# A four-block kernel on one NeuronCore: unread products on TensorE ahead of two stages, and a small step moved up on VectorE

## What is computed

```python
x = x + attn(moe(x, cond, experts, shared))        # top 2 of 8 experts and a shared one
x = x + ffn_quant(lora(x, cond))                   # quantised gate, up and down projection
x = x + retention(cond_linear(x, cond))
x = x + moe_attention(expert_mlp(x, cond))         # 16 experts by token
```

```python
def _gemma_mlp(x, gate_w, up_w, down_w):
    g = einsum('bsh,hi->bsi', x, gate_w)
    u = einsum('bsh,hi->bsi', x, up_w)
    return einsum('bsi,ih->bsh', gelu(g) * u, down_w)

def act_qdq(x):                                    # 16 bits, one scale for the whole tensor
    scale = maximum(max(abs(x)) / qmax, 1e-12)
    return clip(round(x / scale), -qmax - 1.0, qmax) * scale

x = act_qdq(x)
up = act_qdq(x @ lpbq_dequant(w_up).T)
gate = act_qdq(x @ lpbq_dequant(w_gate).T)
```

## Time and profile before

| | us |
|---|---|
| median of 3 runs | 509.73 |
| lowest, highest | 509.29, 510.66 |
| the profiled execution | 510.83 |
| its span, first to last instruction | 509.1 |
| TensorE busy in the span | 443.1 |
| VectorE busy | 414.8 |
| ScalarE busy | 241.4 |
| mean granted clock | 0.95 |

### The profile page before, as it was taken

One profiled execution on the slowest core, in us unless ns is written; L12 is line 12 of the kernel. 1 busy time (PEld: TensorE's weight loads), 2 busy tenths in 40 slices (PEclk: granted clock), 3 DMA queues, 4 the chain that ended last, 5 costly groups with the idle time before them and its releaser, 6 DMA issues.

```text
span 509.1 us, 9168 instructions
## 1 busy us (share of the span) xinstructions
PE 443.1 (87%) x3546; PEld 310.6 (61%) x3546; DVE 414.8 (81%) x902; ACT 241.4 (47%) x422; POOL 54.8 (11%) x69
## 2 busy tenths in 40 slices
PE   2999998999789996800299999999999999999997
PEld 1447998989337963300058987666656655566666
DVE  6879989896578847999853489997798999899786
ACT  5669655564464117998345455336323422422110
POOL 2050000000553001800053000000000000000000
PEclk9999999999999998955589998999999999999999
DMA  7980997850134002403311004391891100000000
GB/s 208 418 324 2 301 345 260 329 196 1 43 109 181 1 1 83 133 32 124 124 50 45 2 0 143 124 320 34 305 316 52 63 7 12 5 6 7 6 5 27
DMA packets 22321, 60.38 MB, mean 119 GB/s; under 512 B 2851, under 2 KB 5286, under 8 KB 22150
## 3 DMA queue, kind: packets, MB, share of 16 engines
q1 hardware_dynamic: 21840, 59.69, 34.0%
q10 hardware_dynamic: 438, 0.11, 0.1%
HBM read 57.56 MB, written 1.18 MB: 115 GB/s over the span
## 4 chain that ended last, share of the span: by engine, by line
PE 37%; DVE 14%; issue 2%; ACT 1%; DVEq 0%; ACTq 0%
PE bk L697 13%; PE bk L705 7%; PE bk L742 5%; PE bk L579 2%; DVE XT L1638 2%; PE bk L625 2%; DVE RA L1666 1%; DVE RA L1458 1%; DVE X L1626 1%; DVE WK L1492 1%; PE bk L729 1%; PE bk L717 1%; PE bk L595 1%; DVE QS L1366 1%; PE bk L608 1%
## 5 line engine op out<-in xcount | busy, mean ns | idle before, releaser
L697 PE MATMUL bk<-X,RB 128*128 128x512 f16 x384 | 94.6, 383 | 0.3 <-DVE X L1626 0.3
L987 ACT ACTIVATE X<-RA 128x512 f16<-128x512 f32 x64 | 40.2, 630 | 100.9 <-DVE RA L1666 83.6
L1638 DVE SCALAR_TENSOR_TENSOR XT<-bk,WK,XT 128x128 f32<-128x128 f32 x192 | 67.1, 349 | 6.0 <-PE bk L742 0.8
L697 PEld LDWEIGHTS bk<-X,RB 128*128 128x128 f16 x384 | 37.1, 99 | 41.7 <-issue 1.1
L705 PEld LDWEIGHTS bk<-RB,X 128*128 128x128 f16 x768 | 48.8, 99 | 15.4 <-issue 0.6
L705 PE MATMUL bk<-RB,X 128*128 128x128 f16 x768 | 53.8, 220 | 0.0
L385 PE MATMUL bk<-X,RC 128*128 128x128 f16 x768 | 48.1, 219 | 3.2 <-DVE RC L1101 2.2
L385 PEld LDWEIGHTS bk<-X,RC 128*128 128x128 f16 x768 | 45.1, 98 | 5.5 <-issue 3.7
L1626 DVE TENSOR_TENSOR X<-RA,X 128x512 f16<-128x512 f32 x64 | 43.8, 685 | 1.3 <-ACT X L987 1.3
L1101 DVE SCALAR_TENSOR_TENSOR RC<-RA,RC 128x1024 f16<-128x1024 f32 x32 | 39.0, 1218 | 6.1 <-ACT RC L807 6.1
L842 ACT ACTIVATE WK<-bk 128x512 f32<-128x512 f32 x48 | 28.5, 595 | 27.2 <-PE bk L385 17.9
(11 more groups left out here) (305 smaller groups left out, 805.4 us busy)
## 6 DMA issues: line engine op xcount, KB each, us to landing
RA<-in_wx SPq DMA_DIRECT2D x32, 768.0 KB, 5.8
RC<-expert_weights SPq DMA_DIRECT2D x22, 256.0 KB, 6.3
X<-in_w SPq DMA_DIRECT2D x8, 512.0 KB, 3.6
RC<-in_w SPq DMA_DIRECT2D x8, 384.0 KB, 5.1
STG<-expert_weights SPq DMA_DIRECT2D x12, 256.0 KB, 6.0
STG<-in_w SPq DMA_DIRECT2D x6, 384.0 KB, 6.7
QT<-expert_weights SPq DMA_DIRECT2D x8, 256.0 KB, 4.6
WBOT<-expert_weights SPq DMA_DIRECT2D x8, 256.0 KB, 4.2
```

Of the source, the lines that this page charges most:

```text
L697: t = e.matmul(BK[m][:, :], P16[:, wp, wo:wo + 128], ZH[:, n % 4, xp, :], start=(e1 == 0 and i == 0), stop=(e1 == 15 and i == 2))
L987: e.activation(ZH[:, r, 0, :], zf[r], ACT.Copy).then_inc(S("z_hi"), 1)
L1638: stt(XT[:, bb_(t_)], bank_o(n)[:, bb_(i)], RW[:, t_, e1:e1 + 1], XT[:, bb_(t_)], ALU.mult, ALU.add).then_inc(S("acc"), 1)
```

## The change

TensorE gets three groups of products whose result nobody reads. Fourteen f32 products of 128 columns of ONES by ONES into bank 7 stand at its start, behind the wait for ONES; four more wait for the first upper half of the tokens (`x_hi`, 1); and eleven f16 products of 512 columns of `FW16` by itself into bank 6 stand between `quant_turn(0)` and the 24 units. On VectorE the theta step with its wait for the column constants stands ahead of `sh_lo(0)` and `x_lo(0)` where it stood behind them.

```diff
         def tensor(e):
             q = Eng(e, by_home)
+            q.wait_ge("const", 1)
+            for _ in range(14):
+                e.matmul(BK[7][:, 0:128], ONES[:, :], ONES[:, :], start=True, stop=True)
+            q.wait_ge("x_hi", 1)
+            for _ in range(4):
+                e.matmul(BK[7][:, 0:128], ONES[:, :], ONES[:, :], start=True, stop=True)
...
             q.wait_ge("x1", 4)
             quant_turn(0)
+            q.wait_ge("fw_lo", 3)
+            for _ in range(11):
+                e.matmul(BK[6][:, :], FW16[:, 0, 0, :], FW16[:, 0, 0:4, :], start=True, stop=True)
...
+            q.wait_ge("col", 16)
+            ts(QS[:, 0:1], col("theta"), 0.0, None, ALU.mult).then_inc(S("theta0"), 1)
             sh_lo(0)
             x_lo(0)
-            q.wait_ge("col", 16)
-            ts(QS[:, 0:1], col("theta"), 0.0, None, ALU.mult).then_inc(S("theta0"), 1)
             sh_lo(1)
             x_lo(1)
```

## The result

| | median us | executions | lowest to highest |
|---|---|---|---|
| before | 509.51 | 6 | 508.56 to 510.66 |
| changed | 505.76 | 6 | 505.13 to 507.29 |

The ratio is 0.993 (0.991 to 0.995): 3.75 us less in the medians. The forecast was 506.8 with a range of 505.1 to 509.4. The profiled execution of the changed kernel took 505.13 with a span of 503.3, and its mean granted clock was 0.956 where before had 0.95.

What follows compares the result with a forecast made beforehand. Half-clock products were taken to limit the shared expert's start, later stages waiting in turn, and VectorE to bound the projections once continuous. Gains 1.8 + 1.15 = 2.95 against the median 509.73 gave 506.8, range 505.1 to 509.4.

Steps and rivals of the forecast that it cites:

- the likeliest case: Both places, at the start and at the quantised projections, give their gains: 506.8 us, chance 0.40.
- the sum: Gains of both places together, 1.8 + 1.15 = 2.95 us, taken from the median of 509.73.
- in the way: Rival at both places: unread products don't raise the clock and only delay, 3.3 us slower, 513.1; chance 0.07.
- in front of a fallen clock: Rival at the quantised projections: clock drops near 194, before the 11; that place gives -0.3, time 508.2; chance 0.12.
- The first place: Shared expert's products at the start: full clock brings the third down product from 21.21 to 19.4; gain 1.8, bounds 0 to 3.0.
- The chain of ScalarE and VectorE: At the start: gelu 0 at 11.5, then 3.7 of steps, sets the first down product at 15.3, against TensorE's own 3.0.
- fewer products are slow: Rival at the start: with seven slow products before, 0.3 of the 1.8 is left; time 508.3; chance 0.19.
- the clock falls back: Rival at the start: idle gap until 8.3 leaves about eight real products at half speed; gain 1.3 there, time 507.3; chance 0.22.
- The second place: Quantised projections, 24 units of three products: maxima start at 198.28 without a gap; gain 1.15, bounds -0.3 to 1.6.
- VectorE is the bound: At the quantised projections from 200.76: 22 maxima in 14.28 without idle, 0.65 each; TensorE needs as much.

Runs made afterwards that it cites:

- narrow ones: The changed kernel with its 18 unread products at the start 8 columns wide instead of 128, the 11 kept: 507.81 against 509.72, ratio 0.9968.
- the relapse: The changed kernel run once more without an edit, profiled execution of 508.94 with late real products: median 505.58 against 510.02, ratio 0.9924.
- the start alone: The changed kernel without the 11 unread products ahead of the projections: 507.9 against 510.16 for the kernel before, ratio 0.9958.
- the eleven alone: The kernel before with only the 11 unread products ahead of the projections added: 507.5, ratio 0.9965 against the kernel before.

## Why the prediction was right, and where it was not

The sign, the range and the likeliest case held: both places gain, and the gains add up. The total came out at 3.75 in the medians where the sum had 2.95.

**Neither in the way nor in front of a fallen clock.** The four didn't delay the start (9.33 against 9.20), though partly by luck: they took 1.16 and not the 0.92 that I had put down, and behind X's upper half at 8.30, as in the trace of before, they would have ended at 9.46. It was there at 7.82, and in all the other traces by 8.0. The eleven ran at full clock in each of the ten traces of kernels that had eleven there: the stage took 20.09 to 20.11 in all of them. The rival in which the clock falls before them was seen in none. Its nearest relative is the kernel without the eleven, in whose trace the clock fell at 192.8, 1.6 us after the transpose: the margin isn't wide.

**The first place, 1.8 forecast.** The pair of traces shows 2.63. The chain of ScalarE and VectorE that I put ahead of the first down product is real: with the theta step back in its place TensorE waits 0.76 for it. But as the bound that keeps the gain at 1.8 of 3.0 it failed. I had the first down product at 15.3 behind the chain, 0.9 after TensorE's own products (9.2 + 24 x 0.216 = 14.4). It came at 14.53, with the chain ready at 14.48 and the 24 products at an end at 14.51, and the third at 18.58 where TensorE alone would have it at 18.40 (9.33 + 42 x 0.216). So nearly all of TensorE's own part was had, less 0.13 for the later start and 0.18 of waiting. The mis-sized step is gelu 0: I gave the theta step 0.45, since I took the landing of the second weight part (2.1 + 6.6) as the next bound at 8.7. That landing comes at different times: in the kernel with the theta step alone ScalarE still waited 0.38 for it, until 8.43; in the changed kernel's profiled execution it was there at 8.26, and as the tokens had landed 0.48 sooner too, the whole 1.0 was had, and gelu 0 started at 10.93, not 11.5. That is 0.6 of the 0.8 that was missing.

But 2.63 isn't what the first place is worth on the whole. Third down products in the traces without wide unread products: 21.21, 20.98, 19.81 and, with narrow ones, 21.07. With them: 18.58, 18.97, 19.39, 18.63, 18.78, 18.94, 18.65; and 21.13 in the relapse. (Two more had other edits at the start: 19.64 with the theta step back, 20.56 without the four.) The ratio of the start alone gives 2.1, its median 2.3. That the forecast of 1.8 is near it is in part luck: the chain was sized too long, and two things that I had as rivals and not in the sum took away from the gain: before, fewer products are slow in some executions (6.79 instead of 8.29 for the same 24), and in the changed kernel the clock falls back in some. By the Trainium skill (TensorE: Matmul & The Clock Gate, "The HAM clock gate") the number of slow products at a start varies with the execution; the rows agree, with 8.29, 7.97 and 6.79, but the variation took a part of the gain and not the whole 1.7 that its smallest count would have.

**The second place, 1.15 forecast.** The pair shows 1.52, and the eleven alone give 1.8 by their ratio, 2.7 by the medians. The step that failed is "VectorE is the bound". I read 22 maxima in 14.28 without idle and took 0.65 for VectorE's own pace. In the changed kernel 24 take 15.36. With 0.69 for one alone, the pitch was (14.28 - 0.69)/21 = 0.647 and is now (15.36 - 0.69)/23 = 0.638. VectorE can be faster than it was: it kept the pace of TensorE, which needs 3 x 0.216 = 0.65, and row after row joined without idle hid that. The ends say the same: the last maximum ends 1.43 after TensorE's last product before (215.04 and 196.33 + 17.28), and 1.44 after it in the changed kernel (210.94 and 193.74 + 15.76), so TensorE set the end of the stage in both. So nearly the whole of what the slow products cost counted, 1.52 of the 1.6 that was the term's upper bound. In other executions it can be more: without the eleven the stage took 21.61, 21.44 and 22.89 in three traces.

**The sum** was right to go by medians. The profiled execution of before was 1.1 above its median, and the trace of after lay 0.6 below its own; a sum read from the pair would have credited the change with 1.6 us of a clock that rose by chance elsewhere.

## What to carry to other kernels

Where TensorE waits for microseconds and then starts a stage that it limits, unread products in that wait can be worth the whole of what the real products at half the clock cost; read the cost from the length of one and the same group of products in several executions, since a single trace shows only one of the cases that occur (8.29, 7.97 or 6.79 for the same 24). Fill the wait up to the first real product and not beyond: without the last four of the start the traced execution had the real ones at half the clock, and eleven too many ahead of the projections cost 2.2 of 2.4 us. Where two engines run in lockstep at one pace, "busy without idle" doesn't say which sets it; look whether the last step of the one comes the same time after the last of the other when the other gets faster (1.43 and 1.44 us here).

## What the hardware showed that I had not expected

Products of 8 columns kept TensorE busy in the rows for 6.14 + 1.88 us and the next 24 still took 7.45; with 128 columns they took 5.34. The busy time ahead of them, as the rows have it, didn't tell which of the two it would be.

VectorE's lower half of the first weight part takes 0.95 or 1.21 for the same work, and the first real products begin with it at 9.2 to 9.4 or at 9.8 to 10.7. It goes with whether GpSimd's five additions have begun. The timeline of the changed kernel:

```profile
7.37 0.95 DVE L1108 SCALAR_TENSOR_TENSOR STG<-STG 128x768 f16<-128x768 f32 x1
7.48 4.43 POOL L1730 TENSOR_TENSOR RB<-RB,C2B 128x128 f32<-128x128 f32 x5 [7.04 <-DVE SM L1098]
```

And that of the kernel with the start alone, where the line of the step is L1105:

```profile
6.98 4.14 POOL L1727 TENSOR_TENSOR RB<-RB,C2B 128x128 f32<-128x128 f32 x5 [6.54 <-DVE SM L1090]
...
7.60 1.21 DVE L1105 SCALAR_TENSOR_TENSOR STG<-STG 128x768 f16<-128x768 f32 x1
...
9.82 5.34 PE L388 MATMUL bk<-X,STG 128*128 128x512 f16 x24 [1.30 <-DVE X L1100]
```

In eight of the fourteen traces VectorE's step begins before GpSimd's or within 0.01 of it and takes 0.95; in the other six GpSimd is 0.47 to 1.9 ahead and it takes 1.21. GpSimd's five took 2.29 in the late execution, where VectorE did its longest steps behind them, and 3.45 to 4.54 in all the others. Of the first of these VectorE steps that holds in all fourteen traces, but no run changed the order on purpose, and the second one, beside the additions, took anything from 0.96 (before, at 10.12) to 1.21. By the Trainium skill (SBUF — State Buffer, "SBUF: two separate sides") a VectorE step with two inputs in SBUF and a GpSimd step that reads SBUF hold one pair of ports in turn, each for the whole instruction, the later one waiting. The rows agree in so far as the later one pays: the 0.26 more of VectorE's step is below the length of one addition (2.29 / 5 = 0.46, an estimate), and the five additions take longer beside VectorE's steps. That the ports are the cause isn't shown by a run. A version in which GpSimd's additions wait for VectorE's first two lower halves suggests itself; it wasn't tried. It would go for executions like the traced one at 508.94, in which a start 1.4 late (10.73 against 9.33) also lost the clock and with it nearly the whole gain of the first place.
